# Sixteen pairs of shared tiles ahead of the experts, and one sum instead of two

## The reference, cut to what matters

```python
x = x + attention(layernorm(x))                      # 4096 tokens x 512
h = layernorm(x)
scores = sigmoid(h @ router_w.T)                     # 16 experts
top4 = top_k(scores + e_bias, 4); w = normalised scores of these 4
for e in range(16):                                  # each token in 4 of them
    g, u = split(h @ gate_up[e].T)                   # 2 x 192
    routed += w[:, e] * (silu(g) * u @ down[e].T)
shared = silu(h @ sg.T) * (h @ su.T) @ sd.T          # all tokens
out = x + routed + shared
```

## Time and profile before

| | us |
|---|---|
| median of 3 timed runs | 1856.76 (1853.92 to 1857.07) |
| profiled execution, own time | 1851.41 |
| its span | 1849.4 |
| PE busy | 1765.4 (95%) |
| DVE, ACT, POOL busy | 1144.6, 883.9, 920.6 |

### The profile page before, as it was taken

How to read it: one execution, slowest core, us unless ns; L and a number is a source line. 1 busy time by engine, 2 the same in 40 slices (tenths; PEclk the granted TensorE clock), 3 DMA queues, 4 the chain that set the end, 5 groups by cost and what they waited for, 6 DMA issues and landing times.

```text
span 1849.4 us, 35292 instructions
## 1 busy us (share of the span) xinstructions
PE 1765.4 (95%) x8536; PEld 899.7 (49%) x8537; DVE 1144.6 (62%) x2172; ACT 883.9 (48%) x1756; POOL 920.6 (50%) x1127
## 2 busy tenths in 40 slices
PE   6899999999999999999999898999999999999995
PEld 5444445455455545554433354545555555555542
DVE  5667787878888888878788646333334433334333
ACT  2367777776777777777777641221222112221210
POOL 3533557676677666676635555033333343333441
PEclk9899999999999999999999999999999999999998
DMA  6423325344534444343344489698888988888889
GB/s 198 123 70 65 90 83 154 102 112 136 157 94 111 137 125 111 117 144 102 101 126 161 154 299 351 181 200 163 161 155 159 167 162 160 154 162 167 161 179 254
DMA packets 255898, 277.76 MB, mean 150 GB/s; under 512 B 57888, under 2 KB 184096, under 8 KB 253024
## 3 DMA queue, kind: packets, MB, share of 16 engines
q0 software_dynamic: 40880, 106.96, 27.4%
q1 hardware_dynamic: 151600, 127.10, 25.2%
q10 hardware_dynamic: 63296, 42.24, 8.2%
HBM read 145.65 MB, written 135.74 MB: 152 GB/s over the span
## 4 chain that ended last, share of the span: by engine, by line
PE 80%; DVE 5%; DMA 5%; ACT 3%; issue 2%; POOL 2%; SPq 1%; ACTq 0%; DVEq 0%; POOLq 0%
PE ps_gu L1986 22%; PE ps_pv L1255 12%; PE ps_exp L1226 10%; PE ps_max L1212 9%; PE ps_y L2003 7%; PE ps_misc L1133 5%; PE ps_y L2013 4%; DVE mx L1002 3%; DMA wts_sb<-second_sum_rows 2%; PE ps_misc L1104 2%; ACT prob L739 2%; PE ps_misc L1144 1%; PE ps_misc L1269 1%; PE ps_misc L1181 1%; PE ps_misc L1120 1%
## 5 line engine op out<-in xcount | busy, mean ns | idle before, releaser
L1002 DVE TENSOR_REDUCE mx<-ps_max 128x2 f32<-128x1024 f32 x512 | 621.4, 1220 | 151.1 <-PE ps_max L1212 131.0
L739 ACT ACTIVATE prob<-ps_exp 128x512 f32<-128x512 f32 x992 | 569.1, 597 | 147.3 <-PE ps_exp L1226 127.2
L1986 PE MATMUL ps_gu<-wts_sb,xT 128*128 x1152 | 399.3, 490 | 1.1 <-POOLq L1644 0.8
L1226 PE MATMUL ps_exp<-qs,ks 98*128 98x512 bf16 x992 | 378.3, 382 | 13.9 <-ACT prob L739 12.6
L1212 PE MATMUL ps_max<-ks,qs 96*128 96x512 bf16 x1024 | 306.4, 380 | 7.3 <-DVE mx L1002 5.3
L1737 ACT ACTIVATE gs<-ps_gu 128x192 f32<-128x192 f32 x176 | 58.3, 331 | 520.7 <-PE ps_gu L1986 322.6
L1685 POOL DMA_INDIRECT out<-yt,idx x72 | 111.7, 1551 | 365.4 <-ACT yt L1747 281.9
L1986 PEld LDWEIGHTS ps_gu<-wts_sb,xT 128*128 128x128 f32 x1152 | 209.7, 190 | 161.3 <-issue 45.9
L1255 PE MATMUL ps_pv<-prob,vs 128*32 128x512 f32 x2048 | 251.5, 604 | 0.2 <-ACT prob L747 0.2
L1226 PEld LDWEIGHTS ps_exp<-qs,ks 98*128 98x128 bf16 x992 | 96.6, 97 | 176.5 <-ACT prob L739 62.0
L1895 DVE SCALAR_TENSOR_TENSOR hid<-ps_gu,wsel,gs 128x192 f32<-128x192 f32 (+2 forms) x216 | 68.4, 344 | 177.3 <-ACT gs L1737 177.3
(11 more groups left out here) (197 smaller groups left out, 2016.5 us busy)
## 6 DMA issues: line engine op xcount, KB each, us to landing
xt<-rows_by_expert SPq DMA_DIRECT2D x296, 64.0 KB
dnr_sb<-in_dnr SPq DMA_DIRECT2D x144, 128.0 KB
xt<-rows_by_expert ACTq DMA_DIRECT2D x280, 64.0 KB
qk_parts<-parts POOLq DMA_DIRECT2D x112, 120.0 KB, 3.6
qs<-qk_parts SPq DMA_DIRECT2D x64, 192.0 KB, 3.0
wts_sb<-in_wts ACTq DMA_DIRECT2D x12, 1024.0 KB, 9.1
x_sb<-in_x SPq DMA_DIRECT2D x16, 512.0 KB, 4.5
qs<-qk_parts SPq DMA_DIRECT2D x64, 128.0 KB, 3.1
```

What stands on the lines that cost most here:

```text
L739: act.activation(prob[:, s, q], ps_exp[:, q % 2], ACT.Exp, scale=SCALE).then_inc(s_exp, 1)
L1002: dve.tensor_reduce(mx[:, k % 2, 4 * s + 2 * p:4 * s + 2 * p + 2], ps_max[:, p], AX_X, ALU.max).then_inc(s_maxd, 1)
L1226: pe.matmul(ps_exp[:, q % 2], ks[0:ROWS + MROWS, kk, s * P:(s + 1) * P], qs[0:ROWS + MROWS, kk, q], start=True, stop=True).then_inc(s_sc, 1)
L1986: mm = pe.matmul(ps_gu[:, i, 0:2 * I], xT[:, i, d], w, start=(d == 0), stop=(d == DC - 1))
```

## The change

All 32 shared tiles come first, as pairs 0 to 15; then the 72 routed pairs; nothing comes behind them. There is one sum, `out`. The y of a shared pair is added to the residual on DVE before it is stored: SP loads the residual rows into `yt` (`load_sum_rows`), DVE adds y from PSUM (`y_sum`), ACT stores the result into `out`. The routed tiles are all added into `out`, still in two chains: each add waits for the one before it in its own chain, and for the adds of the other chain that belong to earlier experts (two tiles of one expert share no token). That number is a new third row of the table `tab`, which POOL reads into a register before each add. Pads now go to spare rows that differ for even and odd tiles of the unused kind (`spare_rows`; `out` has 384 spare rows instead of 128). y of the routed pairs has eight buffers: `yt` and the `xn2` rows of attention, four pairs deep, so the loop runs over four pairs. The work on the tables is spread over pairs 4 to 13, the 12 pads of SP over pairs 6, 8, 10 and 12 (three each; before, six each behind pairs 5 and 6), the weights stand at pairs 0, 3, 5, 9, 11 and 19 (before, 0, 1, 2, 4, 8 and 13). `clear_sums`, `join`, `load_sums` and `both_sums` are gone.

```diff
-EARLY = 20
-        clear_sums()
-    H0 = EARLY // 2
+    H0 = NT // 2
     H1 = H0 + NR // 2
-    H2 = H1 + LATE // 2
+    def y_sb(pair, i):
+        return heads["xn2"][:, pair.par, i, 0:D] if pair.kind == ROUTED and pair.four >= 2 else yt[:, pair.slot(i)]
-        with eng.Fori(0, (L1 - L0) // 2) as r:
-            for i in range(2):
-                body(*around(r * 2 + (L0 + i), r + L0 // 2, i))
+        with eng.Fori(0, (L1 - L0) // 4) as r:
+            for i in range(4):
+                body(*around(r * 4 + (L0 + i), r * 2 + (L0 + i) // 2, i % 2, (L0 + i) % 4))
-    WEIGHTS_AT = {0: 2, 1: 3, 2: 4, 4: 5, 8: 6, H0 + 3: 7}
+    WEIGHTS_AT = {0: 2, 3: 3, 5: 4, 9: 5, 11: 6, H0 + 3: 7}
+        def load_sum_rows(pair):                                             # sync
+            for s, n in done["x2_of"][pair.h]:
+                wait(s, n)
+            for i in range(2):
+                after(wait, s_yst[pair.slot(i)], 16 * pair.q)
+                sp.dma_start(yt[:, pair.slot(i)], rows_of(SUM, pair.t[i])).then_inc(s_yl[pair.slot(i)], 16)
+            if pair.kind == SHARED and pair.par == 1:
+                for ready in (before, pair):
+                    load_sum_rows(ready)
         def add_rows(pair):                                                  # gpsimd
             wait(s_idx, pair.routed + 1)
             for i in range(2):
+                other = pool.value_load(tab[0:1, 2, bass.ds(pair.j[i], 1)], min_val=16, max_val=16 * (NR // 2) + 16)
                 wait(s_y, 2 * pair.h + i + 1)
-                after(wait, s_add[i], 16 * pair.routed)
-                at = idx[:, pair.slot(i):pair.slot(i) + 1]
-                pool.indirect_dma_start(SUM[i], bass.IndirectOffsetOnAxis(ap=at, axis=0), yt[:, pair.slot(i)], None,
+                wait(s_add[i], 16 * pair.routed + 16)
+                wait(s_add[1 - i], other)
+                at = at_sb(pair, i, i + 1)
+                pool.indirect_dma_start(SUM, bass.IndirectOffsetOnAxis(ap=at, axis=0), y_sb(pair, i), None,
                                         compute_op=ALU.add).then_inc(s_add[i], 16)
-                    act.wait_ge(s_add[i], 16 * (pair.routed - 1))            # y_out on scalar
-                act.activation(yt[:, pair.slot(i)], y_of(pair, i), ACT.Copy).then_inc(s_y, 1)
+                    act.wait_ge(s_add[i], 16 * (pair.routed - 2))
+                act.activation(y_sb(pair, i), y_of(pair, i), ACT.Copy).then_inc(s_y, 1)
         def y_sum(pair):                                                     # vector
             dve.wait_ge(s_yp, pair.h + 1)
-            dve.wait_ge(s_both, n)
             for i in range(2):
-                dve.tensor_tensor(late_y(pair, i), y_of(pair, i), sums[:, n, i], ALU.add).then_inc(s_y, 1)
+                dve.wait_ge(s_yl[pair.slot(i)], 16 * pair.q + 16)
+                dve.tensor_tensor(yt[:, pair.slot(i)], y_of(pair, i), yt[:, pair.slot(i)], ALU.add).then_inc(s_y, 1)
+            for h, stage in ((4, pads), (5, tiles_of_experts), (7, tiles_upto), (9, experts_of_tiles), (10, onehots),
+                             (11, first_rows), (13, tables)):
-        "SUM": [out, dram("second_sum_rows", [T + P, D])],
+        "SUM": out,
```

More of the change, by code:

```diff
@@ L469, in gpsimd @@
         pool.wait_ge(s_cstp, 3)
-        def clear_sums():
-            wait(s_zero, 1)
-            wait(s_w, 16 * 5)
-            late = SUM[1][EARLY * P:T].rearrange("(t p) d -> p t d", p=P)
-            pool.dma_start(late, zero[:, 0:D].unsqueeze(1).to_broadcast([P, T // P - EARLY, D])).then_inc(s_clear, 16)
-            for to in range(2):
-                pool.dma_start(SUM[to][T:T + P], zero[:, 0:D]).then_inc(s_clear, 16)
         def rstd(u, mv_, rs_, ready, steps, done):
@@ L1604, in body @@
                 wait(s_tb, 2)
-            for n in range(2):
-                if is_at(pair, 5 + n):
-                    for e in range(POOL_PADS + 6 * n, POOL_PADS + 6 * n + 6):
+            for n in range(4):
+                if is_at(pair, 6 + 2 * n):
+                    for e in range(POOL_PADS + 3 * n, POOL_PADS + 3 * n + 3):
                         pad(e)
@@ L1611, in body @@
                 all_of("xm_stored")
-            if pair.par == 1 and pair.kind == ROUTED:
+            if pair.kind == ROUTED and whole(pair):
                 wait(s_yp, pair.h - 1)
-                for ready in (before, pair):
+                for ready in whole(pair):
                     load_rest(ready)
@@ L1671, in gpsimd @@
             weights_ready(n)
-        all_of("x2_stored", "cleared")
+        all_of("x2_stored")
         for r in range(4):
             wait(s_yst[r], 16 * (H0 // 2))
+        wait(s_tab, 1)
+        for i in range(2):
+            rows = slice(T + i * P // 2, T + (i + 1) * P // 2)
+            pool.dma_start(SUM[rows], zero[0:P // 2, 0:D]).then_inc(s_add[i], 16)
         def add_rows(pair):
@@ L1787, in body @@
             for ready in whole(before):
-                if not ready.both:
+                if ready.kind == SHARED:
+                    store(ready)
+                else:
                     y_out(ready)
-            for ready in whole(before):
-                if ready.kind == SHARED and not ready.late:
-                    store(ready)
-            if before.both:
-                store_late(before)
             last_units(chain, pair, "c")
@@ L1804, in scalar @@
         pairs(act, body)
-        end = Pair(H2 - 1, (H2 - 1) // 2, (H2 - 1) % 2)
-        act.wait_ge(s_y, 2 * end.h + 2)
-        act.sem_inc(s_acg, 1)
-        act.dma_start(rows_of(SUM[0], end.t[1]), late_y(end, 1)).then_inc(s_last, 16)
+        for ready in whole(Pair(H1 - 1, (H1 - 1) // 2, (H1 - 1) % 2)):
+            y_out(ready)
     def vector(dve):
@@ L1858, in tables @@
             step(dve.tensor_tensor(tab[0:1, 0], jt[0:1, 5], jrow[0:1, 2], ALU.add))
+            step(dve.tensor_scalar(spare[:], jt[:, 2], -float(P), float(P), ALU.mult, ALU.add))
+            odd = spare[:, :].rearrange("p (m i) -> p m i", i=2)[:, :, 1]
+            step(dve.tensor_scalar(odd, odd, 2.0, None, ALU.mult))
             dve.tensor_copy(tab[0:1, 1], jt[0:1, 1]).then_inc(s_tab, 1)
@@ L1938, in body @@
             last_units(chain, pair, "c")
-            if is_at(pair, 4):
-                pads()
-                tiles_of_experts()
-            if is_at(pair, 5):
-                experts_of_tiles()
-            if is_at(pair, 6):
-                for s, n in done["qk_stored"]:
-                    dve.wait_ge(s, n)
-                    dve.sem_inc(s_dvg, 1)
-                onehots()
-            if is_at(pair, 7):
-                tables()
-            if before.both:
-                both_sums(before)
-                y_sum(before)
+            for ready in whole(before):
+                if ready.kind == SHARED:
+                    y_sum(ready)
+            for h, stage in ((4, pads), (5, tiles_of_experts), (7, tiles_upto), (9, experts_of_tiles), (10, onehots),
+                             (11, first_rows), (13, tables)):
+                if is_at(pair, h):
+                    stage()
         chain = heads["vector"](dve)
@@ L2034, in tensor @@
         pairs(pe, body)
-        end = Pair(H2 - 1, (H2 - 1) // 2, (H2 - 1) % 2)
+        end = Pair(H1 - 1, (H1 - 1) // 2, (H1 - 1) % 2)
         transpose_h(end)
-        down(end, [None, None])
+        down(end, experts(end))
     own.close()
```

143 lines of the change are left out of this document (53 added, 90 removed).

## The result

The changed kernel takes 1849.56 us (median of 13 runs), the one before 1854.56 on the same chip; the ratio is 0.9963 [0.9954, 0.9973], 6.9 us less. I had forecast 14 us less. One execution of the experiment on the tables (2059.85 us, granted clock 0.845) was in the chip's slower state and is left out.

A forecast was written before the change was run, and what follows sets the result against it. PE bounds the routed loop, busy 50.00 of 50 us. T0 = 1776.8 + 33.1 - 1.8 + 0 + 1.0 = 1809.1; plus 24.3 + 2.0 the span is 1835.4, 14.0 less: 1843 us at the median, range 1831 to 1860.

The forecast's parts named there:

- ring: Rival, shared stage: store of y, residual load and DVE sum turn slower than PE; 1873 to 1895 us; 13%, edge 7%.
- The start, -1.8: Start: without the 3.5 MB of zeros, stores land sooner and PE gains its 1.80 us wait; bounds 0 and 6.3.
- The shared stage, 0: Shared pairs: bytes 0.4 MB less, DMA engines as full, PE's wait the same size; 0 us, at best 8.5 won.
- a sum of PE's waits for `xT` under 3 us: Shared stage, 1080 to 1220 us: a sum under 3 or over 12 us would show part 2 wrong.
- The tables, +1.0: DVE in the shared stage: last table takes 6.6 us behind pair 13, 5.5 covered; 1.0 us lost, bounds 0 and 6.6.
- T0: End of the last double pair (84 and 85): four more pairs, 33.1 us, after 1776.8, with parts 1 to 3: 1809.1.
- The tail, 26.3 behind T0: End: chained adds land 24.3 us behind T0 (22.5 to 31.7), then 2.0 to the end of the span.
- the 0.9: Tail: the register load ahead of each add costs 0.9 us, once in a group; bounds 0 and 1.55.
- The adds in the loop, 0: Routed loop: each chain needs 2 x 5.66 of 16.53 us, spare 5.2 covers one more landing; cost 0, gain 0.
- The rival of the longer loop: Routed loop: the longer loop is fetched again each turn; 16 turns cost 14 us, 1857, no change; 3%.
- my own range: Range of the main forecast (60%): 1835, parts 1 and 5 at better ends, to 1852, part 5 at 31.7.

The follow-up runs named there:

- the experiment on the tables: Changed kernel with table steps on DVE placed otherwise, the last table split behind pairs 12 and 13: 1847.39 us, ratio 0.9945 to the kernel before.
- the two combined kernels: Changed kernel with four single end pairs, weights spread later, four table steps behind pair 11: with zeros put back 1831.44 us (0.9886), without 1834.78 (0.9908).
- four buffers: Changed kernel with four buffers of y instead of eight, a copy waiting for the add two pairs back: 1844.3 us, ratio 0.9954 to before.
- the kernel with x later: Changed kernel with the load of x's fourth tile (512 KB) issued one head later at the start: 1851.07 us, ratio 0.9963 to before.
- the two comparisons: The unchanged changed kernel against the one before, on two chips: 1849.56 us, ratio 0.9963, and 1847.03 us, ratio 0.9950.
- the second profile: Profile of the changed kernel run again as it is, beside another chip's runs of before: 1847.03 us, ratio 0.9950.

## Why the prediction was right, and where its terms were not

The direction held, and the time lies in the range; the gain was half of what I told. The range was 29 us wide, made so for a ring that turned out harmless, and it caught errors in the start and the tail that I hadn't foreseen: that part is luck. By my own steps:

1. The start, -1.8: wrong in sign, and the largest error. The row showed what PE waited for, and that wait did go. What I didn't ask is what SP does once it is 2 to 4 us ahead: its next loads now fall on ACT's stores. Measured at the mark: +1.3 in the first profile, +2.7 on average (76.8 against 74.1); and 3.3 us between the medians of the two combined kernels. The intervals of these two just overlap, but the thirteen profiles point the same way. That taking the zeros away costs this is shown; that SP's two loads among ACT's stores are the reason is read from the rows and not shown by an experiment, since moving one of the two won at most 0.7 us, within the spread. Moving `x_plus_memory` as well wasn't tried.
2. The shared stage, 0: right, and in the main for the reason given, the bytes. The stage up to pairs 10 and 11 is 119.0 us before (one profile) and 120.3 on average since (118.4 to 122.1), 1.3 more and within the spread; it gets shorter only where bytes go out of it (114.3, 113.3 and 111.1). I had named a sum of PE's waits for `xT` under 3 us as the sign that I am wrong. In the first profile there is none between 1080 and 1220 us (in the second 3.7), since the wait now bears the name `hT`: the sign was badly chosen, the interval between products is what to read. The ring did show in that form, DVE waiting for `yt<-out`, five times, 2.0 us at most: a part of the same stall, not one of its own.
3. The tables, +1.0: 1.3 in each profile in which they are in one piece behind pair 13 (an interval of 17.85 instead of 16.53). A sum takes 0.69 us, four of them 2.8, a little above my bound of 2.6.
4. T0: not in my sum was that the last weights fall on the first routed pairs, now as before: 6.6 us there in the first profile, some 2.4 on average, where before had 2.8 (0.99 and 1.77 over two intervals). The first profile is no fair picture of that.
5. The tail, 26.3 behind T0: 26.9 to 27.9 in nine profiles. The register load costs nothing: the first two adds are 1.86 us apart as in the earlier trace rows, so the 0.9 was too much. In its place came one link of 7.36 where I had 5.66, and a last link of 5.53 where I had 4.8. No run keeps two tensors with the new order of pairs, so what the end won is read from these marks alone.
6. The adds in the loop, 0: right, with four buffers as well. The eight buffers of the change win nothing here. The rival of the longer loop didn't come either: PE is busy for all of 1300 to 1800 us.

The ends of my own range don't follow from the parts named beside them. Parts 1 and 5 at their better ends give 1842.8 - 4.5 - 1.8 = 1836.5, and 1835 needs part 3 at 0 as well; part 5 at 31.7 gives 1850.2, and 1852 needs part 1 at 0.

One more piece is not explained. From the mark to pair 0 it took 1000.4 us before, and 1000.0 to 1003.9 since (1008.3 in the kernel with x later). It is lost at the end of attention, between 1040 and 1080 us, as two windows of PE alone show (busy, clock, DMA share, GB/s), first before, then after:

```profile
1040.00:1060.00 20.00, 16.23 (x104) 0.97 0.77 278
1060.00:1080.00 20.00, 16.82 (x86) 0.94 0.62 198
```

```profile
1040.00:1060.00 20.00, 18.43 (x109) 0.83 0.73 254
1060.00:1080.00 20.00, 13.24 (x74) 0.88 0.63 205
```

```profile
1048.18 1.03 PE L1229 MATMUL ps_exp<-qs,ks 98*128 98x512 bf16 x2 [1.05 <-issue]
...
1050.00 3.64 PE L1243 MATMUL ps_pv<-prob,vs 128*32 128x512 f32 x16
```

Here and in most other profiles the granted clock falls to its lower level (1.2 GHz) behind a wait of PE of 1 to 3.8 us; sixteen products then take 3.64 us where they take 1.92 at 1057.24. Why these waits lie otherwise from kernel to kernel stays open. With 2.8 us for it (the mean of the ten profiles without zeros), 4.5 for the start, 0.3 for the tables, 1.1 for the tail and 1.3 for the shared stage, the forecast of -14 becomes -4.0. It is reckoned against the profile of before, whose own time (1851.41) lay 3.2 us below the median of its 13 runs, while that of after (1850.0) lay near its median (1849.56): -7.2 by medians. Measured are -5.0 and -8.6 by the medians of the two comparisons.

## What to carry to other kernels

When a transfer is taken away, ask what its queue's followers will do with the time: here an engine that ran ahead issued its next loads among another engine's stores, and with 3.5 MB of useless zeros written the kernel was 3.3 us faster (medians of the two combined kernels). The stall under full DMA engines didn't go with the wait's name: take transfers out of the whole full stretch, since what was only moved within it made the stall again, later. A chain of dependent adds to DRAM costs 5.5 to 5.9 us a link here, so finish the last items one by one where a chain sets the end.

## What the runs showed of the hardware

- The same start varies: the mark lay between 74.64 and 78.45 us in the ten profiles without zeros, though PE's first product came at 10.93 to 11.39 in all. Terms under 3 us want marks from several profiles, not one.
- An indirect add that waits for the one before it takes 5.84 us from issue to issue on average when its chain is alone, and 5.5 to 5.8 behind T0 beside a second chain, but for one of 7.36: there is no sign that the two chains slow each other.
- Issuing four stores of 120 KB took ACT 3.0 to 3.7 us beside small loads, and 5.5 to 6.8 where two transfers of 512 KB from SP fell among them.
- The store of 120 KB issued by SP at 38.10 landed in 2.6 us; four of this size from ACT, in the full stretch of the second profile from 54 us on, landed in 4.1 at the median. The Trainium skill, DMA: Bandwidth & Descriptors, section Anatomy of one DMA, has a fit for DMAs issued by GpSimd, 2.0 us and the bytes over 436 GB/s. By it 120 KB would take 2.3 us, an estimate. These stores are issued by SP and ACT, so it is not their fit; the first lies near it, the four do not.
- The loop's body is twice as long as before, and PE pays nothing for it: it is busy for all of the 500 us from 1300 to 1800.
